# A gated cross-attention block on one core: x1 stays in the PSUM bank of y until ScalarE moves it out

## The reference

```
xn   = (x - mean(x)) / sqrt(var(x) + 1e-5)                 # per row
q, k = ctx @ Wq.T + bq, ctx @ Wk.T + bk                    # 512 x 128
x1   = x + tanh(g0) * xn @ softmax(q @ k.T).T              # 512 x 512
z    = (x1 - mean(x1)) / sqrt(var(x1) + 1e-5), normalised once more,
       times ln_weight, plus ln_bias
out  = x1 + tanh(g1) * (z @ sign(W).T * max|W| * gamma + beta)
```

## Time and profile before

| what | value |
|---|---|
| median of 3 runs | 133.01 us (132.58 to 133.08) |
| the profiled execution | 132.29 us |
| its span, first to last instruction | 130.8 us |
| mean granted clock of TensorE | 0.977 of full speed |
| busy, share of the span | PE 91%, DVE 73%, POOL 71%, ACT 66% |

### The profile page before, as it was taken

How to read it: one execution, slowest core, us unless ns; L and a number is a source line. 1 busy time by engine, 2 the same in 40 slices (tenths; PEclk the granted TensorE clock), 3 DMA queues, 4 the chain that set the end, 5 groups by cost and what they waited for, 6 DMA issues and landing times.

```text
span 130.8 us, 1869 instructions
## 1 busy us (share of the span) xinstructions
PE 119.5 (91%) x558; PEld 94.7 (72%) x558; DVE 94.8 (73%) x187; ACT 86.8 (66%) x185; POOL 92.3 (71%) x106
## 2 busy tenths in 40 slices
PE   5968999999999999948999999999999999999830
PEld 4517688888888878826888888878888888887730
DVE  1148699897988992479764992898859738997672
ACT  4243999999998889037797797179997940334300
POOL 3006899916329989998363799994649999839790
PEclk9999999999999999996899999999999999999996
DMA  3949999735532500247450502357000202220043
GB/s 80 246 141 393 392 388 296 306 76 152 186 89 74 160 0 5 83 147 250 165 160 0 160 0 85 116 205 228 13 3 3 74 11 80 80 80 0 0 182 139
DMA packets 10649, 17.15 MB, mean 131 GB/s; under 512 B 1808, under 2 KB 2576, under 8 KB 10640
## 3 DMA queue, kind: packets, MB, share of 16 engines
q1 hardware_dynamic: 9920, 17.04, 38.3%
q10 hardware_dynamic: 720, 0.00, 0.3%
HBM read 12.59 MB, written 4.19 MB: 128 GB/s over the span
## 4 chain that ended last, share of the span: by engine, by line
PE 53%; ACT 17%; POOL 14%; DVE 6%; issue 4%; POOLq 1%; ACTq 1%; DVEq 1%
PE ps_y L372 23%; PE ps_ffn L385 14%; POOL x L863 5%; PE ps_turn L339 4%; PE ps_score L332 4%; ACT prob L507 3%; PE ps_ffn L310 3%; POOL x L868 3%; PE ps_score L446 3%; ACT prob L513 2%; ACT k_hi L496 2%; POOL xt_lo L851 2%; ACT x_sb L544 2%; ACT q_hi L496 1%; DVE neg_max L640 1%
## 5 line engine op out<-in xcount | busy, mean ns | idle before, releaser
L863 POOL TENSOR_TENSOR x<-x,shift 128x512 f32<-128x512 f32 x16 | 21.1, 1320 | 8.1 <-ACT unread L538 8.1
L851 POOL TENSOR_TENSOR xt_lo<-xt_raw,xt_hi 128x512 fp32r<-128x512 f32 x16 | 21.6, 1350 | 7.3 <-ACT xt_hi L519 4.2
L685 DVE SCALAR_TENSOR_TENSOR zw<-x,neg_mean,ln_w 128x512 f32<-128x512 f32 x16 | 19.4, 1209 | 0.4
L868 POOL TENSOR_TENSOR x<-x,ffn 128x512 f32<-128x512 f32 x14 | 18.9, 1356 | 0.0
L372 PE MATMUL ps_y<-pt_hi,xt_hi 128*128 128x512 f32 x64 | 18.9, 418 | 0.0
L507 ACT ACTIVATE prob<-ps_score,neg_max 128x512 f32<-128x512 f32 x14 | 9.5, 681 | 13.8 <-DVE neg_max L640 13.8
L372 PE MATMUL ps_y<-pt_hi,xt_lo 128*128 128x512 f32 x64 | 18.4, 411 | 0.0
L555 ACT ACTIVATE zt_hi<-ps_turn 128x512 fp32r<-128x512 f32 x16 | 9.5, 594 | 12.9 <-PE ps_turn L339 12.9
L711 DVE SCALAR_TENSOR_TENSOR ffn<-ps_ffn,rstd,gain 128x512 f32<-128x512 f32 x15 | 11.2, 746 | 9.1 <-POOL x L868 4.1
L385 PE MATMUL ps_ffn<-w_sign,zt_hi 128*128 128x512 f32 x60 | 17.2, 408 | 0.5 <-DVE ffn L711 0.5
L372 PE MATMUL ps_y<-pt_lo,xt_hi 128*128 128x512 f32 x64 | 17.6, 396 | 0.0
(11 more groups left out here) (160 smaller groups left out, 241.5 us busy)
## 6 DMA issues: line engine op xcount, KB each, us to landing
xt_raw<-in_x_t_dram SPq DMA_DIRECT2D x16, 256.0 KB, 3.0
out_dram<-x SPq DMA_DIRECT2D x15, 256.0 KB, 2.0
ctx_sb<-in_ctx_t_dram SPq DMA_DIRECT2D x8, 256.0 KB, 6.8
x_sb<-in_x_dram SPq DMA_DIRECT2D x8, 256.0 KB, 5.0
ctx_sb<-in_x_dram SPq DMA_DIRECT2D x8, 256.0 KB, 6.2
w_raw<-in_weight_t_dram SPq DMA_DIRECT2D x4, 256.0 KB, 8.2
ln_w<-in_ln_weight_dram SPq DMA_DIRECT2D x1, 256.0 KB, 7.6
gain<-in_gamma_dram SPq DMA_DIRECT2D x1, 256.0 KB, 8.6
```

Of the source, the lines that this page charges most:

```text
L685: nc.vector.scalar_tensor_tensor(out=zw[:, t, :], in0=x1[:, t, :], scalar=neg_mean2[:, t:t + 1], in1=ln_w[:, :], op0=ALU.add, op1=ALU.mult)\
L851: nc.gpsimd.tensor_tensor(xt_lo[:, t, :, :], xt_raw[:, t, :, :], xt_hi[:, t, :, :].bitcast(f32), ALU.subtract).then_inc(xt_lo_done, 1)
L863: nc.gpsimd.tensor_tensor(x1[:, t, :], x1[:, t, :], shift[:, :], ALU.add).then_inc(x1b_done, 1)
L868: nc.gpsimd.tensor_tensor(x1[:, t, :], x1[:, t, :], ffn[:, t % 2, :], ALU.add)\
```

## The change

`add_y` writes x1 back into the PSUM bank of y, without the row bias (its wait for the store is gone, and its wait for `x_biased` becomes one for `y_bias` having been made and one for x). `centre` reads the bank; a bias for each row drops out of a centred row. Behind it a small DVE instruction makes `neg_moved2` = -mean - y_bias. The new ACT step `move_x1` copies the bank into SBUF's x1 and adds `y_bias` on the way; it waits for `centre` and for the store. `square_x1` reads that copy with the new shift. PE's waits for a free `ps_y` bank are now for `x1_moved`. The `bias_x` instructions, 16 of them, are gone; there are 16 of `move_x1`, at other places of ACT's order. `centre(b, 3)` stands earlier in DVE's order. `y_bias` is kept for two samples.

```diff
@@ PE
 def turn_prob(b, t):                     # t >= 2, sample b > 0
-                    pe.wait_ge(x1_done, T * (b - 1) + t + 1)
+                    pe.wait_ge(x1_moved, T * (b - 1) + t + 1)
 def attend(b, t):
                 if t >= 2:
-                    pe.wait_ge(x1_done, T * b + t - 1)
+                    pe.wait_ge(x1_moved, T * b + t - 1)
@@ ACT
+            def move_x1(b, t):
+
+                act.wait_ge(zw_done, T * b + t + 1)
+                act.wait_ge(out_stored[t], 16 * (b + 1))
+                nc.scalar.activation(x1[:, t, :], ps_y[t % 2][:, :], ACT.Identity,
+                                     bias=y_bias[:, b % 2, t:t + 1]).then_inc(x1_moved, 1)
+
             def square_x1(b, t):
 
-                act.wait_ge(mean2_done, T * b + t + 1)
+                act.wait_ge(x1_moved, T * b + t + 1)
+                act.wait_ge(shift2_done, T * b + t + 1)
...
-            def bias_x(b, tiles):
-                act.wait_ge(ln1_done, 2 * b + 2)
-                for t in tiles:
-                    nc.scalar.activation(x_buf[b % 2][:, t, :], x_buf[b % 2][:, t, :], ACT.Identity,
-                                         bias=y_bias[:, t:t + 1]).then_inc(x_biased, 1)
             def back(b):
+                move_x1(b, 0)
                 exps(b + 1, 0)
                 stats_x(b + 1, 0)
+                move_x1(b, 1)
                 exps(b + 1, 1)
                 normalise(b + 1, 0)
                 turned_ffn_hi(b, 0)
...
                 exps(b + 1, 3)
+                move_x1(b, 2)
                 normalise(b + 1, 2)
...
                 turned_prob_hi(b + 1, 1)
+                move_x1(b, 3)
                 turned_prob_hi(b + 1, 2)
...
                 turned_ffn_hi(b, 3)
-                bias_x(b + 1, (0, 1))
                 split_xt(b + 1, 3)
-                bias_x(b + 1, (2, 3))
...
             round_qk(3, 1)
-            bias_x(0, range(T))
@@ ACT, sample 3
-            for t in range(T):
-                turned_ffn_hi(B - 1, t)
-                square_x1(B - 1, t)
+            move_x1(B - 1, 0)
+            move_x1(B - 1, 1)
+            turned_ffn_hi(B - 1, 0)
+            square_x1(B - 1, 0)
+            move_x1(B - 1, 2)
+            turned_ffn_hi(B - 1, 1)
+            square_x1(B - 1, 1)
+            move_x1(B - 1, 3)
+            turned_ffn_hi(B - 1, 2)
...
@@ DVE
             def add_y(b, t):
-                dve.wait_ge(out_stored[t], 16 * (b + 1))
-                dve.wait_ge(x_biased, T * b + t + 1)
+
+                dve.wait_ge(x_in[b % 2][t], 16 * (b // 2 + 1))
+                dve.wait_ge(ln1_done, 2 * b + 2)
                 dve.wait_ge(y_ready, T * b + t + 1)
-                nc.vector.scalar_tensor_tensor(out=x1[:, t, :], in0=ps_y[t % 2][:, :],
+                nc.vector.scalar_tensor_tensor(out=ps_y[t % 2][:, :], in0=ps_y[t % 2][:, :],
...
             def centre(b, t):
                 dve.wait_ge(mean2_done, T * b + t + 1)
-                nc.vector.scalar_tensor_tensor(out=zw[:, t, :], in0=x1[:, t, :], scalar=neg_mean2[:, t:t + 1],
+                nc.vector.scalar_tensor_tensor(out=zw[:, t, :], in0=ps_y[t % 2][:, :], scalar=neg_mean2[:, t:t + 1],
                                                in1=ln_w[:, :], op0=ALU.add, op1=ALU.mult)\
                          .then_inc(zw_done, 1)
+                nc.vector.tensor_scalar(neg_moved2[:, t:t + 1], neg_mean2[:, t:t + 1], 1.0,
+                                        y_bias[:, b % 2, t:t + 1], ALU.mult, ALU.subtract)\
+                         .then_inc(shift2_done, 1)
@@ DVE, back(b)
                 add_y(b, 3)
                 mean_x1(b, 3)
+                centre(b, 3)
                 stats_x(b + 1, (3,))
                 turned_ffn_lo(b, 2)
                 scale_ffn(b, 0)
                 turned_prob_lo(b + 1, 0)
-                centre(b, 3)
```

More of the change, by code:

```diff
@@ L103, in flamingo_block_kernel @@
         y_back = sb("y_back", [P, T])
-        y_bias = sb("y_bias", [P, T])
+        y_bias = sb("y_bias", [P, 2, T])
         sum2 = sb("sum2", [P, T])
         neg_mean2 = sb("neg_mean2", [P, T])
+        neg_moved2 = sb("neg_moved2", [P, T])
         sq_sum2 = sb("sq_sum2", [P, T])
@@ L176, in flamingo_block_kernel @@
         power1_done = sem("power1_done")
-        x_biased = sem("x_biased")
+        x1_moved = sem("x1_moved")
+        shift2_done = sem("shift2_done")
         later_zeroed = sem("later_zeroed")
@@ L531, in stats_x @@
                                      accum_out=sq_sum1[:, t:t + 1]).then_inc(square1_done, 1)
+            def move_x1(b, t):
[3 more added lines that the diff above has]
+                                     bias=y_bias[:, b % 2, t:t + 1]).then_inc(x1_moved, 1)
             def square_x1(b, t):
-                act.wait_ge(mean2_done, T * b + t + 1)
+                act.wait_ge(x1_moved, T * b + t + 1)
+                act.wait_ge(shift2_done, T * b + t + 1)
                 if T * b + t > 0:
                     act.wait_ge(square2_done, T * b + t)
-                nc.scalar.activation(unread[:, 2, :], x1[:, t, :], ACT.Square, bias=neg_mean2[:, t:t + 1],
+                nc.scalar.activation(unread[:, 2, :], x1[:, t, :], ACT.Square, bias=neg_moved2[:, t:t + 1],
                                      accum_out=sq_sum2[:, t:t + 1]).then_inc(square2_done, 1)
-            def bias_x(b, tiles):
-                act.wait_ge(ln1_done, 2 * b + 2)
-                for t in tiles:
-                    nc.scalar.activation(x_buf[b % 2][:, t, :], x_buf[b % 2][:, t, :], ACT.Identity,
-                                         bias=y_bias[:, t:t + 1]).then_inc(x_biased, 1)
             def turned_prob_hi(b, t):
@@ L631, in _ @@
                 back(b)
-            for t in range(T):
-                turned_ffn_hi(B - 1, t)
-                square_x1(B - 1, t)
+            move_x1(B - 1, 0)
[7 more added lines that the diff above has]
+            turned_ffn_hi(B - 1, 2)
+            square_x1(B - 1, 2)
+            turned_ffn_hi(B - 1, 3)
+            square_x1(B - 1, 3)
         @block.vector
@@ L894, in scale_x @@
                     pool.wait_ge(ln1_done, 2 * b + 1)
-                    nc.gpsimd.tensor_tensor(y_bias[:, :HALF], neg_mean1[:, :HALF], y_scale[:, b % 2, :HALF], ALU.mult)\
+                    nc.gpsimd.tensor_tensor(y_bias[:, b % 2, :HALF], neg_mean1[:, :HALF], y_scale[:, b % 2, :HALF], ALU.mult)\
                              .then_inc(scale1_done, 1)
-                nc.gpsimd.tensor_tensor(y_bias[:, cols], mv1[:, cols, 0], y_back[:, cols], ALU.mult)\
+                nc.gpsimd.tensor_tensor(y_bias[:, b % 2, cols], mv1[:, cols, 0], y_back[:, cols], ALU.mult)\
                          .then_inc(ln1_done, 1)
```

## The result

The changed kernel takes 136.2 us (median of 4 runs, 135.84 to 136.63). Beside it the kernel before took 132.8 us; the ratio is 1.027, with a 95% interval of 1.021 to 1.032. The profiled execution took 136.41 us, its span is 134.9 us, 4.1 above that of before.

A forecast was written before the change was run, and what follows sets the result against it. The prediction took PE to bound the kernel except in round 0, set by ACT, the gain and POOL. Its terms 0 + 0.1 + 1.5 + 1.2 made +2.8 us, giving 135.8 us at the median, range 132.9 to 137.8.

The forecast's parts named there:

- Round 0: Stretch until turn_ffn(1,0): the gain 1.3 us late, won back by faster shift, var and centre; sum about 0.
- Round 1: From there to attend(2,0): ACT about 1.6 us late at turn_prob(2,3), against 1.5 us lost before to the lower clock; +0.1 us.
- Round 2: Until attend(3,0), the main term: moves waiting for centres make ACT late, and turn_prob(3,3) waits for move_x1(2,3); +1.5 us.
- Sample 3: In `last`, attend(3,2) waits for centre(3,0) and move_x1(3,0), behind scale_ffn(2,3) and POOL; +1.2 us.
- The pieces: Instruction times: centre from PSUM 0.75 us, add_y into PSUM 0.75 us, move_x1 like ACT's evictions with a bias, 684 ns.
- Edits costed at nothing: The store's wait in ACT's queue, the earlier centre(b,3), and SP's loads waiting for x1_done were taken to add no time.
- the clock falls behind the new wait of 1.2 us: Slower rival: the wait ahead of attend(3,2) makes the clock fall, +1.5 us, 137.3 us; chance 0.15.
- The faster case: Rival: gain not late in round 0, ACT's idle time takes the moves of rounds 1 and 2; 131.7 or 130.2; chance 0.1.
- The case of no change: Rival: DVE's relief and ACT's lateness cancel, 0.1 us each at turn_prob(3,3) and attend(3,2); 133.3 us; chance 0.1.
- Slow work in PSUM: Rival: add_y and centre in PSUM both take 1.31 us, +4.5 us, 140.3 us; chance 0.05.

The follow-up runs named there:

- Experiment 3: The changed kernel with move_x1(0,1) put behind exps(1,1), normalise(1,0) and turned_ffn_hi(0,0), in round 0 alone: 134.3 us, 1.021 of the kernel before.
- experiment 2: The changed kernel with two swaps in ACT's order: exps(b+1,0) and exps(b+1,1) ahead of move_x1(b,0) and move_x1(b,1): 133.8 us, 1.011 of the kernel before.
- Experiment 1: The changed kernel with a second copy of the bank, into an unread buffer, ahead of each move_x1: 141.7 us, 1.072 of the kernel before.
- experiment 4: Mean and centre of tile 0 put ahead of scale_ffn(b,3) in DVE's order: 132.5 us in the changed kernel, 129.2 us in the kernel before.
- Experiment 5: The changed kernel with mean_x1(3,0) and centre(3,0) alone ahead of scale_ffn(2,3): 134.8 us, 1.020 of the kernel before.
- experiment 6: The kernel before with PE's bank waits on zw_done and centre(b,3) earlier: 133.1 us; a second kernel with centre(b,3) earlier alone: 132.6 us.
- experiment 7: The kernel before with copies of x1 from SBUF to an unread buffer at the moves' places in ACT's queue, and centre(b,3) earlier: 139.4 us, 1.060.
- experiment 8: The changed kernel with centre of tile 0 ahead of scale_ffn(b,3) and moves later in ACT's order: 129.6 us, 0.984 of the kernel before.

## Why the prediction was right

The forecast was 135.8 us, the measured time 136.2. The mechanism holds, and so do its places: PE waits for `move_x1` at `turn_prob(b+1,3)` and at attend(3,2), because the moves lengthen ACT's queue and a loop over ACT, POOL and DVE. That the total is so close is in part luck. The sum was +2.8 us; the profiles give +3.55 with the start out, the medians +3.4. Round 0 came out 0.4 us below its term and the other three stages 0.5, 0.4 and 0.2 above, so the misses cancel in part. And the forecast was added to a median of 133.0, where the kernel before measured 132.8 beside the changed one.

- **Round 0 (forecast 0, measured -0.4).** exps(1,1) was to start at 34.05 and did at 34.65 - 0.55 = 34.10. The lateness of the gain was to be 1.3 us and was 1.0: 40.26 - 0.55 = 39.71 against 38.70. What I missed is that DVE had idled for 0.50 us ahead of the second step of `stats_x(1,2)` before, and does not now. The chain closes with that: +1.0, less 0.3 each for `shift` and `var` and 0.7 for the centre, is -0.4. That PE's own lateness fits into the gap held: 0.90 us of it are left. Experiment 3 shows the cause. I gave a time for the path over w_max alone, where experiment 2 shows a second wait behind it, in `turned_ffn_lo(0,0)`; both hang on the same move, so the sum is the same.
- **Round 1 (+0.1, measured +0.6).** The reasoning held: the clock stayed up, the four matmuls took 1.17 us instead of 1.93, and PE waited 0.15 + 0.54 + 0.73 us instead. The size was off by half a microsecond, and the term that was too small is ACT's lateness at `turn_prob(2,3)`, forecast at 1.6 us. From turn_ffn(1,0) to `turn_prob(2,3)` it is 15.58 us (59.57 to 75.15); in the kernel before the same path took 13.42 in round 2 at full clock (86.01 to 99.43) and 14.96 in round 1 with the slow clock. So ACT makes the path 2.2 us longer than PE's own, and 0.6 of it is left over the 1.5 of the clock.
- **Round 2 (+1.5, measured +1.9).** The main term. It was built step by step against PE's times of before. It was 0.4 us too small from its first step on: centre(2,0) started 0.7 us later than before (85.73 - 0.55 against 84.46), where 0.4 was forecast, because `add_ffn(1,1)` on POOL was 0.7 late and not 0.5. What the term describes without naming it is a loop: move(b,0), ACT's queue, `split_xt`, POOL, `scale_ffn(b,3)`, centre(b+1,0), of 26.97 us against 25.07 for PE's round. Experiment 1 shows that the moves lie in it at full length, experiment 4 that it closes through `scale_ffn`.
- **Sample 3 (+1.2, measured 1.20 us of wait, +1.4 in the table).** The two numbers are the same wait, as a bracket and as PE's loss. Experiment 5 takes it away by the one step named.
- **The pieces.** Centre 749 ns and `add_y` into PSUM 754, both forecast at 0.75 us; the move 691 ns.
- **Edits costed at nothing.** The store's wait in ACT's queue never shows: no `move_x1` is released by a transfer. centre(b,3) placed earlier cost nothing in the changed kernel: in its rounds PE never waits for `scale_ffn`. By itself in the kernel before it made 1.5 us of such waits, and the time stayed the same only because the clock did not fall (experiment 6).
- **The rivals.** That the clock falls behind the new wait of 1.2 us did not happen: the next four matmuls took 1.17. That was not certain, since in experiment 7 it fell behind a wait of 1.13. The faster case failed at both of its conditions: the gain was 1.0 us late, and ACT was late at `turn_prob(3,3)`. But its premise, that ACT has room for the moves, was right in another order (experiment 8). The case of no change wanted 0.1 us at each of the two late places, and they were 1.9 and 1.4. Slow work in PSUM is ruled out by 749 and 754 ns.

The Trainium skill (VectorE: DVE Perf Modes, section on the TRN2 errata) prices a PSUM source at 62 cycles of 0.96 GHz above an SBUF source, by estimate 0.065 us for each centre. This case's traces show less, 0.017 us: 749 ns as the mean from PSUM, against 732 for the shortest from SBUF. For elementwise work on a matmul's output the Trainium skill (same page, rules for kernel authors) says to accept the PSUM source, or to copy to SBUF first if many operations follow. Here one centre follows, and it takes 1209 ns as a mean from SBUF in the kernel before and 749 from PSUM; no run here has many.

## What to carry to other kernels

An operation that is swapped one for one on an engine with a third of its time idle is not free: its place decides, and what it waits for holds all that stands behind it in the queue. Ask of each new wait which instruction of another engine stands next behind it, and follow the loop once around all engines; here the loop through ACT, POOL and DVE became longer than the bounding engine's own round, 26.97 against 25.07 us. When spans of a few microseconds' difference are compared stage by stage, first take out what differs ahead of the change. And before a change is dropped, try the order again: the same operations in another order went from 136.2 to 129.6 us, and one step moved in the kernel before gave the same within what these runs can tell (129.2).

## What the runs showed of the hardware

- The length of a gap alone did not decide whether TensorE's clock fell. Before, behind 2.28 us without a matmul, PE's next four took 1.93 us, and the granted clock over 59.8 to 64.2 us was 0.61 of full speed, so most of it was at the lower of the two levels (1.2 GHz). In experiment 7 a gap of 2.32 us at the same place was followed by four that took 1.19, at a granted clock of 1.00 from 60 to 64 us; near the end of the same execution a gap of 1.13 us was followed by 1.60 and 1.91, at 0.59 from 127.6 to 130.8 us. Gaps of 1.65 (experiment 6) and 0.90 us were followed by 1.18 and 1.17. PE's rows of experiment 7:

```profile
60.74 0.66 PE L341 MATMUL ps_turn<-ident,zw 128*128 128x128 f32 x4 [2.32 <-DVE zw L707]
61.16 1.19 PE L374 MATMUL ps_y<-pt_hi,xt_hi 128*128 128x512 f32 x4
...
127.64 1.60 PE L387 MATMUL ps_ffn<-w_sign,zt_hi 128*128 128x512 f32 x4 [1.13 <-DVE ffn L733]
129.04 1.91 PE L387 MATMUL ps_ffn<-w_sign,zt_lo 128*128 128x512 f32 x4
```

- The kernel before itself does not run alike each time. Of its 13 executions beside experiments 1, 2 and 4, nine had a mean granted clock of 0.976 to 0.981 and spans of 130.3 to 131.3 us, three had 0.987 or 0.988 and 129.8 to 130.1, and one had 0.992 and 129.3. That the difference is the fall behind the gap is not shown, as only one of its executions has a trace; if it is, the change costs some 5 us against an execution in which the clock stays up, by estimate: 3.55 plus the 1.5 that PE lost from 59.81 to 64.24 us against the same matmuls a round later (86.42 to 89.31).
- Writing x1 back into its own PSUM bank costs DVE nothing (754 against 749 ns), though the row that reads the sum out behind it went from 82 to 142 ns.
- POOL gains when DVE's second SBUF operand goes: `xt_lo` from 1350 to 1294 ns as a mean of 16. In the five kernels with the centre's source in SBUF this mean is 1345 to 1350 ns, in the seven with it in PSUM 1290 to 1298.
